# The bias of a fourth head moves from VectorE to TensorE in a banded attention kernel

## The reference

```python
q, k, v = x @ Wq.T, x @ Wk.T, x @ Wv.T          # [B, S, 32, 16], rotary on q and k
scores  = einsum('bhid,bhjd->bhij', q, k) * 16 ** -0.5
bias    = where(causal & (i - j < 256), learnable_bias[h, i - j], 0)
scores  = where(causal, scores + bias, -inf)
m       = maximum(max_j scores, offset[h])
p       = exp(scores - m);  denom = sum_j p + exp(offset[h] - m)
out     = (p @ v / denom) @ Wo.T
x       = layernorm(x + out)
x       = layernorm(x + linear(mxfp4(x), mxfp4(weight)) + ffn_bias)
```

## Time and profile before

| | |
|---|---|
| median of 3 runs | 1916.54 us (1915.15 to 1916.69) |
| the profiled execution | span of 1914.6 us from its first to its last instruction; the page gives no other time for it |
| mean granted TensorE clock over the span | 0.946 of full speed |
| busy, share of the span | PE 91%, PEld 46%, DVE 73%, ACT 46%, POOL 13% |
| phase 2 | from the first bias matmul at 417.9 us to the last at 1628.1 us |
| instructions at L663 (TensorE bias) | 1920 matmuls and 1920 weight loads |
| instructions at L1131 (VectorE bias) | 320, 140.6 us busy |

### The profile page before, as it was taken

The page is one execution under the profiler, slowest core; times in us unless marked ns, Lnnn a source line. Parts: engine busy times, 40 slices in busy tenths (PEclk is TensorE's granted clock), DMA queues, the critical chain, the costliest instruction groups (busy, mean ns, idle before and its releaser), DMA issues.

```text
span 1914.6 us, 35268 instructions
## 1 busy us (share of the span) xinstructions
PE 1736.2 (91%) x9768; PEld 880.6 (46%) x9776; DVE 1404.3 (73%) x4121; ACT 878.6 (46%) x1148; POOL 256.0 (13%) x122
## 2 busy tenths in 40 slices
PE   7999999489989998998998998999899999787762
PEld 3444444125545554554554554555455554343331
DVE  2444444698878887887887887888788771679996
ACT  2333333115545554554554554555455556344442
POOL 4333233300000000000000000000000000034442
PEclk9999999669999999999998999999999999899996
DMA  5445345714332522442334323252253201111111
GB/s 196 160 140 169 132 169 150 193 31 80 62 60 46 110 46 47 93 76 47 76 63 77 70 54 64 49 103 46 47 105 64 46 24 45 61 55 66 66 66 44
DMA packets 124695, 157.81 MB, mean 82 GB/s; under 512 B 14928, under 2 KB 80528, under 8 KB 124240
## 3 DMA queue, kind: packets, MB, share of 16 engines
q1 hardware_dynamic: 124496, 155.45, 34.3%
HBM read 104.15 MB, written 50.46 MB: 81 GB/s over the span
## 4 chain that ended last, share of the span: by engine, by line
PE 68%; issue 13%; DVE 12%; POOL 3%; ACT 1%; DMA 1%; DVEq 1%; SPq 0%; POOLq 0%; ACTq 0%
PE ps L643 14%; PE ps L680 14%; PE ps L658 13%; PE ps L619 12%; PE ps L663 12%; DVE junk L1118 2%; DVE mx L1111 2%; PE ps L768 2%; POOL probs L987 1%; PE ps L690 1%; DVE ps L1131 1%; POOL probs L1028 1%; DMA attn<-wvT 1%; DVE stats L1303 1%; POOL k_stack L1032 1%
## 5 line engine op out<-in xcount | busy, mean ns | idle before, releaser
L856 ACT ACTIVATE probs<-ps 128x1024 f32<-128x1024 f32 (+3 forms) x768 | 615.8, 813 | 562.4 <-PE ps L663 309.3
L1118 DVE CUSTOM_DVE_ANT_0 junk<-ps,bias_q 128x384 bf16<-128x384 f32 (+2 forms) x1024 | 503.7, 502 | 137.3 <-PE ps L643 124.1
L663 PE MATMUL ps<-bias_r,ident_r 128*128 (+3 forms) x1920 | 539.9, 368 | 0.0
L643 PE MATMUL ps<-k_stack,q_stack 96*128 96x384 bf16 (+3 forms) x1536 | 504.8, 347 | 35.0 <-DVE mx L1118 17.1
L658 PE MATMUL ps<-q_stack,k_stack 99*128 99x512 bf16 (+3 forms) x1536 | 496.8, 333 | 22.3 <-issue 19.8
L1111 DVE TENSOR_REDUCE mx<-ps 128x1 f32<-128x128 f32 (+3 forms) x768 | 365.0, 485 | 40.9 <-PE ps L643 32.5
L663 PEld LDWEIGHTS ps<-bias_r,ident_r 128*128 128x128 f32 x1920 | 338.0, 195 | 64.2 <-issue 1.7
L619 PE MATMUL ps<-attn 128*128 128x512 f32 x768 | 332.6, 596 | 10.7 <-DMA attn<-hT 9.8
L680 PE MATMUL ps<-probs,v_sb 128*32 128x512 f32 (+3 forms) x3072 | 327.3, 498 | 4.4 <-ACT probs L856 4.4
L643 PEld LDWEIGHTS ps<-k_stack,q_stack 96*128 96x128 bf16 x1536 | 143.4, 98 | 393.6 <-DVE mx L1118 197.7
L619 PEld LDWEIGHTS ps<-attn 128*128 128x128 f32 x768 | 146.7, 191 | 195.8 <-issue 195.8
(11 more groups left out here) (88 smaller groups left out, 1050.2 us busy)
## 6 DMA issues: line engine op xcount, KB each, us to landing
q_stack<-q_parts SPq DMA_DIRECT2D x192, 128.0 KB, 4.1
v_dram<-v_sb SPq DMA_DIRECT2D x32, 512.0 KB, 2.7
v_sb<-v_dram SPq DMA_DIRECT2D x32, 512.0 KB, 9.1
q_parts<-q_stack SPq DMA_DIRECT2D x96, 128.0 KB, 1.9
k_parts<-k_stack SPq DMA_DIRECT2D x96, 128.0 KB, 2.0
k_stack<-k_parts SPq DMA_DIRECT2D x32, 384.0 KB, 7.1
attn<-hT SPq DMA_DIRECT2D x8, 1024.0 KB, 6.0
k_stack<-k_parts SPq DMA_DIRECT2D x32, 256.0 KB, 7.8
```

The source lines that it names most:

```text
L643: pe.matmul(ps_ring[:, use.bank, 0:c1 - c0], q_stack[0:STACK, b, hl, I * P:(I + 1) * P], k_stack[0:STACK, b, hl, c0:c1], start=True, stop= ...
L663: mm = pe.matmul(ps_s[:, u % 2, hh, 0:bw], ident_r[:, :], rhs, start=False, stop=(s == 1))
L856: act.activation(probs[:, (u // 2) % 3, 2 * pr:2 * pr + 2, 0:w], ps_s[:, pr, :, 0:w], ACT.Exp).then_inc(exp_done, 1)
L1118: ins = dve.tensor_tensor_reduce(out=junk[:, use.bank, 0:c1 - lo], in0=ps_ring[:, use.bank, lo - c0:c1 - c0], in1=bias_q[:, hl, BAND - t0 ...
```

## The change

Head 3 gets its bias as the other three do: two FP32R matmuls onto its scores, in every banded tile. The VectorE addition, the copy of head 3's bias on GpSimd and the two semaphores between the engines go. `bias_r` grows from three heads to four and takes more SBUF than `bias_k` gave back, so several small tensors share room with others: the fp32 identity becomes a view of the FP32R one, its first form is built in `o_sb`, the parts of the shifts lie in the unused fourth row of `work`, and the scales of the quantisation lie in `mx` and `e_off`.

```diff
-        bias_k = sb("bias_k", [P, 2, BAND])
-        bias_r = sb("bias_r", [P, 2, 2, HG - 1, BAND], FP32R)
+        bias_r = sb("bias_r", [P, 2, 2, HG, BAND], FP32R)
-        ident = sb("ident", [P, P])
+        ident = ident_r[:, :].bitcast(FP32)
+        ident_new = o_sb[:, 0, 0:P]
-        shift_parts = sb("shift_parts", [HG * NB, PARTS, P], BF16)
-        shift_rest = sb("shift_rest", [HG * NB, P])
+        shift_rest = work[0:HG * NB, 3, 0:P]
+        shift_parts = work[0:HG * NB, 3, P:P + PARTS * P // 2].bitcast(BF16).rearrange("p (s t) -> p s t", s=PARTS)
-        amax = sb("amax", [P, 4 * NQ])
...
+        by_quarter = mx[:, :, :, :, :].rearrange("p a h i s -> p (a h i s)")
+        amax, scale4, pow2 = [by_quarter[:, 4 * NQ * i:4 * NQ * (i + 1)] for i in range(3)]
+        by_half = e_off[:, :, :].rearrange("p b n -> p (b n)")
+        qscale, qinv = [by_half[:, 4 * NQ * i:4 * NQ * (i + 1)] for i in range(2)]
...
-                    pe.wait_ge(bias_split, 3 * (g + 1))
+                    pe.wait_ge(bias_split, 2 * (g + 1))
...
-                    on_pe = bw and hl < HG - 1
+                    on_pe = bw > 0
...
-                    if hl == HG - 1:
-                        mm.then_inc(last_head_scored, 1)
...
             def exp_unit(g, b, n, u):
                 c, J, i0, w = tile_cols(u // 2)
-                if u % 2 and u // 2 in BANDED:
-                    act.wait_ge(biased, n * NBAND + BANDED.index(u // 2) + 1)
...
-                pool.tensor_copy(hi, bias_in[:, 0:HG - 1, ::-1]).then_inc(bias_split, 1)
-                pool.wait_ge(bias_split, 3 * g + 1)
-                pool.tensor_tensor(lo, bias_in[:, 0:HG - 1, ::-1], hi.bitcast(FP32), ALU.subtract)\
+                pool.tensor_copy(hi, bias_in[:, :, ::-1]).then_inc(bias_split, 1)
+                pool.wait_ge(bias_split, 2 * g + 1)
+                pool.tensor_tensor(lo, bias_in[:, :, ::-1], hi.bitcast(FP32), ALU.subtract)\
                     .then_inc(bias_split, 1)
-                pool.tensor_copy(bias_k[:, slot, :], bias_in[:, HG - 1:HG, ::-1]).then_inc(bias_split, 1)
...
-            def add_bias(g, n, T):
-
-                b0, bw = band_cols(T)
-                if T == 0:
-                    dve.wait_ge(bias_split, 3 * (g + 1))
-                dve.wait_ge(last_head_scored, n * NT + T + 1)
-                tile = ps_s[:, 1, 1:2, 0:bw]
-                dve.tensor_tensor(tile, tile, bias_k[:, bass.ds(g % 2, 1), b0:b0 + bw],
-                                  ALU.add).then_inc(biased, 1)
...
-                        if u % 2 and u // 2 in BANDED:
-                            add_bias(g, n, u // 2)
```

More of the change, by code:

```diff
@@ L74, in band_cols @@
     return b0, max(0, min(BAND - b0, w))
-BANDED = [T for T in range(NT) if band_cols(T)[1]]
-NBAND = len(BANDED)
 def max_units():
@@ L361, in build @@
         bias_split = sem("bias_split")
-        last_head_scored = sem("last_head_scored")
-        biased = sem("biased")
         ring_filled = sem("ring_filled")
@@ L543, in phase2 @@
                     if b == 1 and not last:
-                        wait_then_address(bias_split, 3 * (g + 1))
+                        wait_then_address(bias_split, 2 * (g + 1))
                         load_bias_k(g + 1)
@@ L961, in _ @@
             pool.memset(ext_q[:, P - 1 + BIAS:EXT], 0.0).then_inc(ext_zeroed, 1)
-            pool.memset(ident[:, :], 0.0).then_inc(ident_set, 1)
+            pool.memset(ident_new, 0.0).then_inc(ident_set, 1)
             pool.wait_ge(ident_set, 1)
-            pool.affine_select(out=ident[:, :], in_=ident[:, :], compare_op=ALU.not_equal, fill=1.0,
+            pool.affine_select(out=ident_new, in_=ident_new, compare_op=ALU.not_equal, fill=1.0,
                                base=0, pattern=[[-1, P]], channel_multiplier=1).then_inc(ident_ready, 1)
             pool.wait_ge(ident_ready, 1)
-            pool.tensor_copy(ident16[:, :], ident[:, :]).then_inc(ident_ready, 1)
+            pool.tensor_copy(ident16[:, :], ident_new).then_inc(ident_ready, 1)
             pool.wait_ge(ident_ready, 2)
@@ L976, in _ @@
             pool.memset(eps[:, :], EPS).then_inc(ident_ready, 1)
-            pool.tensor_copy(ident_r[:, :], ident[:, :]).then_inc(ident_ready, 1)
+            pool.tensor_copy(ident_r[:, :], ident_new).then_inc(ident_ready, 1)
             pool.wait_ge(rope_loaded, 32)
@@ L1002, in take_bias @@
                 lo = bias_r[:, slot, 1, :, :].rearrange("p a h c -> p (a h) c")
-                pool.tensor_copy(hi, bias_in[:, 0:HG - 1, ::-1]).then_inc(bias_split, 1)
-                pool.wait_ge(bias_split, 3 * g + 1)
-                pool.tensor_tensor(lo, bias_in[:, 0:HG - 1, ::-1], hi.bitcast(FP32), ALU.subtract)\
+                pool.tensor_copy(hi, bias_in[:, :, ::-1]).then_inc(bias_split, 1)
+                pool.wait_ge(bias_split, 2 * g + 1)
+                pool.tensor_tensor(lo, bias_in[:, :, ::-1], hi.bitcast(FP32), ALU.subtract)\
                     .then_inc(bias_split, 1)
-                pool.tensor_copy(bias_k[:, slot, :], bias_in[:, HG - 1:HG, ::-1]).then_inc(bias_split, 1)
             take_bias(0, 0)
-            pool.wait_ge(bias_split, 3)
+            pool.wait_ge(bias_split, 2)
             pool.wait_ge(rot_lo, 32)
```

## The result

The changed kernel takes 1989.9 us (median of 4, 1989.4 to 1990.5), the kernel before 1916.6: a ratio of 1.0384, 95% interval [1.0369, 1.0398]. It is 73.3 us slower; forecast were 64.7, a time of 1981 in a range of 1960 to 2007.

A forecast was written before the change was run, and what follows sets the result against it. TensorE was taken to bound phase 2: 90.3 us of bias matmuls added less 25.6 given back is +64.7 on the 1914.6 us span, 1979.3, and 1.9 more for the median gives 1981 us. Range 1960 to 2007.

The forecast's parts named there:

- What bounds the kernel: Phase 2: TensorE bounds it, with under 1 us of a 36.9 us batch in which it has nothing to do.
- Case B: Rival for phase 2: nothing is given back, TensorE's waits only move; 1916.5 + 90.3 = 2007 us; chance 0.08.
- case C: Rival: VectorE paces chunk 0 of phase 2, hiding its four added pairs; whole changes by +11, 1927 us; chance 0.08.
- case D: Rival: TensorE is not full, all added pairs are hidden and 25.6 us won back; 1891 us; chance 0.06.
- The price of the pairs: On TensorE, head 3's ten bias pairs add 2.75 us a batch, 88.0 in 32 batches; bounds 84.2 and 91.2.
- the 2.3 us for the slow clock: At group starts TensorE runs near 1.2 GHz, so tile 0's added pair takes 0.64 instead of 0.35: 2.3 us more.
- The give-back: TensorE's waits in phase 2 that go with VectorE's additions: 3.2 us a group, 25.6 in eight; bounds 0 and 38.
- the term 1.9 a group: Tile c=0, J=3: TensorE's gaps before L643 go, 0.55 us a batch, 0.27 in a group's first; 1.9 a group.
- The starts of batches: There the exponential waits for an addition queued behind the shifts; TensorE's waits of 0.33, 0 and 0.15 go: 0.5 a group.
- the ends of groups: TensorE stands 1.18 us there, waiting at L697 and L680; 0.8 a group taken as won, 0.38 kept as a rest.
- the prediction's own sign of an error: It would be wrong if TensorE's gaps in tile c=0, J=3 stay with VectorE idle, so not waits for the ring.
- ScalarE's 194 us of waits for VectorE: ScalarE waits 194 us for the additions; counted at nothing beyond the gaps TensorE shows, as ScalarE is busy half the time.

The follow-up runs named there:

- experiment 1: The changed kernel without head 3's two bias matmuls, so head 3 gets no bias and VectorE's additions are gone too: 1901.9 us.
- Experiment 3: The changed kernel with one bias matmul for head 3 instead of two, the low part left out: 1947.6 us.
- Experiment 7: The changed kernel with both bias parts and the identity in bf16 instead of FP32R, for all four heads: 1932.4 us.
- experiment 2: The changed kernel with head 3's bias pairs kept and VectorE's additions and their two semaphores put back as well: 1997.9 us.
- Experiments 5 and 6: The changed kernel with matmuls for the maxima moved out of tile c=0, J=3: pushed later, 2004.2 us; one pulled earlier to J=1, 1989.2 us.

## Why the prediction was right

**What bounds the kernel: right.** TensorE's own gaps, not the chain's shares, gave the size. The chain had VectorE at 7.1% and hand-overs at 7.4%; taking VectorE's additions away was worth 14.5 us, 0.8% (experiment 1). Two slips on the way did no harm: there are six stalls between 500 and 1500 us in the chain, 19.8 us, and not five of 17; and 4 x 4,608 columns at 0.22 us for 512 are 7.9 us and not 8.1, which leaves 1.2 us of a batch free by that addition and not under 1. Case B (no give-back, 2007) is out by the same run, case C (VectorE paces chunk 0, 1927) and case D (TensorE is not full, 1891) by the result.

**The price of the pairs: right, and to the last digit by luck.** Forecast 88.0 at full clock and 90.3 in all; measured 88.0 from experiment 1 to the changed kernel, with the pairs' pieces at the prices of the earlier trace rows. Experiment 3 halves it (42.3). But inside a group a batch takes 36.4 us in experiment 1 and 39.3 after, so ten pairs cost 2.9 us there and not 2.75, 92 in 32 batches. In the first batch of a group they cost less: its first two tiles, at the slow clock in part, take 8.8 us in experiment 1 and 8.6 after, with two pairs more. So the 2.3 us for the slow clock are not seen in these two executions, and two small errors cancel.

The estimate by the Trainium skill's "TensorE: Matmul & The Clock Gate", section "Back-to-back issue gap", 73 us, was too low for FP32R. Experiment 7 shows where the formula holds: with a bf16 identity a 384-column pair takes 0.33 us, and N/2.4 + 2.5 ns twice is 0.325. The same section of the Trainium skill gives that formula for an isolated matmul and about 81 ns at 128 columns for a stream with weight loads; this trace does not agree, since its bf16 pairs of 128 columns take 0.11 to 0.12 us in such a stream.

**The give-back: right in kind, mis-sized.** "Sum given back: 1.9 + 0.5 + 0.8 = 3.2 us a group, 25.6 in eight" took all of the gaps for VectorE's load. Measured is 14.5 by experiment 1, and 88.0 - 73.3 = 14.7 against the changed kernel; with the pairs in place the additions are worth 8.0 (experiment 2). So the 8.6 us by which the forecast was short are 11 too many given back, less 2.3 too many for the pairs. The kernel before and experiment 1 give TensorE the same matmuls in the same order, so that their starts can be laid side by side. Tile c=0, J=3, from its first score matmul to that of the next tile, goes from 2.77 us to 2.49 in the second to fourth batch of a group, and stays at 2.48 in the first: 6.7 us in all, where the term 1.9 a group had 15.2. This is the term that failed. The starts of batches gave 0.33 and 0.16 us a group, as forecast, and the ends of groups between 0.3 and 1.1 us, 5.3 in seven, as forecast too (0.8 each); the rest of the difference lies in the first two tiles of the groups, at the slow clock in part, and varies from group to group.

The part that stayed is one gap of about 0.27 us in each of the 30 batches that have maxima, 8.1 us. It is the round trip of the ring shown above, and with it the prediction's own sign of an error, gaps of the earlier trace rows that stay, came true for one of the two. Experiments 5 and 6 bear it out as far as they go: with fewer maxima in J=3 its gap closes. The gaps that open elsewhere in them stand beside a busy VectorE and say nothing of the round trip. Whether a fourth bank would close it was not tried; all eight banks of PSUM are in use.

**The rest: right but for the clock of one group.** ScalarE's 194 us of waits for VectorE were worth nothing beyond the places above. GpSimd's longer first part, 1464 ns for 1150, is hidden behind 951.6 us of waits for its transfer. VectorE waits 288 us for L638 between 500 and 1600 us, where it waited 145 for L643. The waits of that line's weight load for VectorE's maxima shrank by a tenth only, from 222 to 203 us. The granted clock is as before inside the groups, but the last group began with 0.50 from 1496.3 to 1499.7 us in the kernel before, and has 1.00 from 1560 to 1570 in the changed one, in the one execution of each that was profiled. And from the last score matmul to the end it is 285.9 us where it was 286.8. Phase 2 starts 1.8 us later, behind the last rotation of phase 1, in the one execution that was profiled; no cause was looked for.

**Case D.** The Trainium skill's "Perfetto Trace Analysis", section "Identifying the Most-Contended Engine", would have TensorE judged by the floating-point work it does against its peak, and by its weight-load share. The second is 54% of a batch; the first was not worked out. Here the weight-load share misleads: an engine with 54% of weight loads took on 88 us of matmuls and got 88 us longer. The start-to-start distances had said so.

## What to carry to other kernels

Before work moves from one engine to another, read each one's true gaps from its own starts: a chain that runs through an engine says that it hands over last, not that its work is on the path, and here 131 us less of it were worth 14.5. Then separate the gaps by what the engine waited for did just before it took up the awaited buffer. Where it was idle, the buffer's round trip makes the gap, and relieving the engine does not close it; where it was busy with something else, its load does. And when TensorE is the bound, look at the operand type of its cheapest-looking matmuls first: two bf16 parts in place of two FP32R ones saved 57.5 us, more than any division of the work between engines that was tried here.

## What the runs showed of the hardware

A weight load of a 128 x 128 FP32R identity takes 191 ns at the median, a bf16 one 98. In the FP32R kernels the price of a short pair hangs on the matmul before it: a pair of 128-column FP32R matmuls takes 0.23 us behind a 128-column matmul and 0.17 behind a 512-column one, the bf16 pair 0.11 to 0.12 behind either. At 384 columns the difference is 0.35 against 0.33. That the longer load shows where the matmul before it is too short to cover it fits these numbers; no run changed the load alone.
